# Expert stage of a GNN + MoE kernel: the fetch of output rows waits for the scatter ahead of it only where a table says so

## The chip, the cores and the metric

The kernel runs on one core of one Trainium2 chip. The metric is the device time of one execution in microseconds (us). The engines are PE (matmul), DVE (vector), ACT (scalar), POOL (GpSimd) and SP (SyncE, which here only issues transfers). Each has its own instruction queue, worked off in order. Queues wait for each other through semaphores; a transfer raises its semaphore by 16 when it has landed.

## The reference

```python
x = x + _L0_gnn_ref(_layernorm(x), edge_index, ...)      # graph attention, 3125 nodes, 50000 edges
x = x + _L0_ffn_ref(_layernorm(x)[None], ...)[0]
# _L0_ffn_ref: x [3125, 1024] float32, E = 8 experts, F = 512, top_k = 2
top_v, top_i = jax.lax.top_k(gate_scores, top_k)
gate_probs = jax.nn.softmax(top_v, axis=-1)
comb = jnp.sum(jax.nn.one_hot(top_i, E) * gate_probs[..., None], axis=-2)
h = jax.nn.gelu(jnp.einsum('bsd,edf->ebsf', x, W1) + b1[:, None, None, :], approximate=False)
eo = jnp.einsum('ebsf,efd->ebsd', h, W2) + b2[:, None, None, :]
out = jnp.einsum('ebsd,bse->bsd', eo, comb)
```

Each node goes to exactly two different experts, and the two results, weighted by their gates, are added to its row.

## The kernel before

The first two thirds of the time are the graph layer. Then a routing block sorts the 6250 pairs (node, expert) by expert and pads every expert to a multiple of 128 slots, at least one tile. There are XTILES = 56 tiles of P = 128 slots. `tokT` holds the node of every slot (3125 and above for an empty one, which the transfers skip), `gateT` its gate. A chain of small DVE steps on one partition (lines 1454 to 1482) makes a table `x_i` with a column per tile: row 0 a word with the tile's expert and flags (first tile of an expert, and so on), rows 1 to 3 further numbers. An engine reads an entry into a register with `tile_value` (line 1534).

The expert stage (from line 1515) runs over the 56 tiles in order. Tile i has parity p = i % 2, and i = 2j + p; most buffers are double by parity. What each queue does for a tile:

- SP (line 1563 on): loads the tile's output bias, broadcast to 128 partitions (`b_t`, 512 KB, line 1569), and, once for each of the later experts, the weights of the expert three ahead (`w_f`, two transfers of 2 MB, line 1286), when the buffer is free.
- POOL, in `body`: `gather(i + 2)` (lines 1271 to 1280) copies a column of node numbers to `xi` and issues the indirect load of 128 normed rows; `put(i - 1)` waits until DVE is done with tile i - 1 and issues the indirect scatter of its 128 rows of 4 KB to `out` (line 1594); `fetch(i)` waits for the scatter of tile i - 1 to land, copies the node numbers (line 1586) and issues the indirect load of the 128 rows of `out` into `y[p]` (line 1588).
- PE: `first(i)` (24 matmuls of 512 columns, line 1695), the first half of `second(i - 1)` (12, line 1710), the turning of the gathered input of tile i + 1 (line 1762), the second half of `second(i - 1)` (12), the turning of h (line 1721).
- ACT: gelu (line 1656), the high half of h (1658), the copy of the turned input (1648) and of the turned h (1664); at an expert's first two tiles also two pieces each of the high half of new weights (1293).
- DVE: bias on h (line 1628), the low half of h (1631), then `take(i - 1)`: `x_o = x_o / 64 + b_t` (line 1618) and `y = x_o * gate + y` (line 1621); at an expert's first two tiles also two pieces each of the low half of new weights (1300).

A fetch must see what an earlier scatter wrote to the same row. Within one expert every node has at most one slot; a row that tile i fetches was written by a neighbouring tile only if that tile belongs to another expert. The semaphores are `s_st[p]` (scatters of parity p), `s_y[p]` (fetches), `s_eo` (takes), `s_tr` (inputs turned). `wait_apart` (line 118 on) gives a wait an instruction of its own.

The lines that the change works on:

```python
def fetch(i, j, p):
    if not early(i, 1):
        wait_apart(pool, s_met, s_st[1 - p], 16 * (j + p))
    pool.tensor_copy(xi[:, 2 + p, :], at1(tokT, i)).then_inc(s_xo, 1)
    wait_apart(pool, s_met, s_xo, i + 1)
    pool.indirect_dma_start(out=y[:, p, :], ..., in_=out[:, :], ...).then_inc(s_y[p], 16)
```

Of the kernel before, what the change touches and what calls it, by code (L numbers as in the profile page):

```python
# [31 lines left out]
I32 = mybir.dt.int32  # L32
U32 = mybir.dt.uint32
F16 = mybir.dt.float16
ALU = mybir.AluOpType
# [22 lines left out]
XTILES = (PAIRS + NX * P - 1) // P  # L58
# [37 lines left out]
def early(i, n):  # L96

    return isinstance(i, int) and i < n
# [19 lines left out]
def wait_apart(eng, met, sem, value):  # L118


    if not isinstance(value, int):
        eng.lower_val(value)
    eng.wait_ge(met, 1)
    eng.wait_ge(sem, value)
# [42 lines left out]
def program(nc, x, src, dst, W, att_src, att_dst, bias, Wp, sim, temp, W1, b1, W2, b2, out):  # L167
# [12 lines left out]
    ctx = ExitStack()  # L180
# [4 lines left out]
    def sbuf(c, name, shape, dt=F32):  # L185
        return c.enter_context(nc.sbuf_tensor(name, shape, dt))
# [4 lines left out]
    s_met = sem("always_met")  # L191

    with ctx:
# [18 lines left out]
        gateT = sbuf(ctx, "gate_of_slot", [P, XTILES])  # L212


        x_i = sbuf(ctx, "tile_experts", [1, 4, XTILES], I32)


        edge_ctx = ExitStack()
# [1083 lines left out]
        with ExitStack() as c:  # L1302
# [18 lines left out]
            base = sbuf(c, "base", [ROWS, NX, BLOCKS + 1])  # L1321
# [10 lines left out]
            slot_f = sbuf(c, "slot_f", [ROWS, 2, BLOCKS])  # L1332
            dif = sbuf(c, "dif", [ROWS, 3, BLOCKS])
            tile_r = sbuf(c, "tile_r", [1, XTILES])
            xcmp = sbuf(c, "xcmp", [1, XTILES, NX - 1])
            xe_f = sbuf(c, "xe_f", [1, XTILES + 1])
            x_t = sbuf(c, "x_t", [1, 5, XTILES + 1])
# [10 lines left out]
            with nc.Block() as block:  # L1348
# [7 lines left out]
                @block.gpsimd  # L1356
                def _(pool):
                    pool.memset(strict[:, :], 1.0).then_inc(s_k, 1)
                    pool.iota(block_of[:, :], pattern=[[0, 2], [1, BLOCKS]], base=-BLOCKS, channel_multiplier=0,
                              allow_small_or_imprecise_dtypes=True).then_inc(s_k, 1)  # L1360
                    pool.iota(tile_r[:, :], pattern=[[P, XTILES]], base=0, channel_multiplier=0,
                              allow_small_or_imprecise_dtypes=True).then_inc(s_k, 1)
                    pool.wait_ge(s_k, 3)
                    pool.affine_select(out=strict[:, :], in_=strict[:, :], compare_op=ALU.is_gt, fill=0.0, base=0,
                                       pattern=[[1, ROWS]], channel_multiplier=-1).then_inc(s_k, 1)
                    pool.wait_ge(s_tok, 1)
                    gather(pool, 0, 0)
                    gather(pool, 1, 1)
# [13 lines left out]
                def _(dve):  # L1382
# [60 lines left out]
                    dve.tensor_tensor(in_tile, iota16[0:ROWS, 0:XTILES].unsqueeze(1).broadcast_to([ROWS, PLACES, XTILES]),  # L1443
                                      slot_p[:, 0, :].unsqueeze(2).broadcast_to([ROWS, PLACES, XTILES]), ALU.is_equal).then_inc(s_tile, 1)
                    dve.wait_ge(s_tile, 1)
                    dve.wait_ge(s_k, 4)
                    dve.tensor_tensor(at_tile[:, :, 0, :], in_tile,
                                      block_of[:, :].unsqueeze(2).broadcast_to([ROWS, PLACES, XTILES]), ALU.mult).then_inc(s_part[0], 1)
                    for n in range(2):
# [22 lines left out]
                    dve.tensor_tensor(x_t[:, 0, now], xe_f[:, now], xe_f[:, ago], ALU.not_equal)  # L1472
                    dve.tensor_scalar(ahead[:, :], xe_f[:, :], float(NX - 3), None, ALU.is_lt)
                    link(dve.tensor_scalar(x_t[:, 1, now], xe_f[:, now], float(NX - 2), None, ALU.is_lt))
                    link(dve.tensor_tensor(first[:, now], x_t[:, 0, now], x_t[:, 1, now], ALU.mult))
                    dve.memset(ahead[:, 0:1], 0.0)
                    link(dve.tensor_tensor(ahead[:, now], first[:, now], ahead[:, now], ALU.mult))
# [19 lines left out]
                @block.tensor  # L1497
                def _(pe):
                    pe.wait_ge(s_oh, 1)
                    pe.wait_ge(s_k, 4)  # L1500
                    flat = both[:, :, :].rearrange("r b e -> r (b e)")
                    pe.matmul(b_ps[0:ROWS, 0, 0:BLOCKS * NX], ones[0:ROWS, 0:ROWS], flat, start=True, stop=True).then_inc(s_mm, 1)
                    pe.matmul(b_ps2[0:ROWS, 0, 0:BLOCKS * NX], strict[:, :], flat, start=True, stop=True).then_inc(s_mm, 1)

                    for n, to in enumerate((inv_ps, gate_ps)):
                        for part in s_part[2 * n:2 * n + 2]:
                            pe.wait_ge(part, 1)
                        for j in range(PLACES):
                            if n == 0 and j % BLOCKS == 0:
                                pe.wait_ge(s_row, j // BLOCKS + 1)  # L1510
                            ins = pe.matmul(to[:, 0:2 * XTILES], at_row[:, j, :], at_tile[:, j, 2 * n:2 * n + 2, :], start=(j == 0), stop=(j == PLACES - 1))
                        ins.then_inc(s_inv, 1)


        with expert_ctx, ExitStack() as c:
# [17 lines left out]
            def tile_value(eng, n, i, **bounds):  # L1533
                return eng.value_load(x_i[:, n, i:i + 1] if isinstance(i, int) else x_i[:, n, bass.ds(i, 1)], **bounds)
# [27 lines left out]
            with nc.Block() as block:  # L1562
# [18 lines left out]
                def _(pool):  # L1581
                    def fetch(i, j, p):

                        if not early(i, 1):
                            wait_apart(pool, s_met, s_st[1 - p], 16 * (j + p))
                        pool.tensor_copy(xi[:, 2 + p, :], at1(tokT, i)).then_inc(s_xo, 1)  # L1586
                        wait_apart(pool, s_met, s_xo, i + 1)
                        pool.indirect_dma_start(out=y[:, p, :], out_offset=None, in_=out[:, :],
                                                in_offset=bass.IndirectOffsetOnAxis(ap=xi[:, 2 + p, :], axis=0),
                                                bounds_check=NODES - 1, oob_is_err=False).then_inc(s_y[p], 16)  # L1590
# [220 lines left out]
```

## Time and profile before

| | |
|---|---|
| median of 3 runs | 2454.21 us |
| lowest, highest | 2448.95, 2456.05 us |
| the profiled execution, its own time | 2455.99 us |
| its span, first to last instruction | 2454.2 us |
| mean granted TensorE clock | 0.903 of full speed |
| PE, DVE, ACT, POOL busy | 2006.4 (82%), 1517.5 (62%), 1115.4 (45%), 709.3 (29%) us |
| moved by transfers | 489.14 MB, 199 GB/s on average |

The time is that of the whole execution, the span what the profile covers of it. Busy time is time in which an engine works on an instruction; instructions that only wait, branch, load a register or issue a transfer from SP are not counted. The granted clock is the share of the full TensorE clock that the chip allows at a time: it has two levels, 1.2 and 2.4 GHz. The chain that ended last is followed back from the last instruction, at each step to what released it. In a timeline, the text in brackets is how long the engine had been idle before the instruction and what ended the wait. A transfer issued by POOL shows as a DMA_INDIRECT of about 1 us, the time that POOL's engine needs to issue it; its landing is seen in what waits for it.

### The profile page before, as it was taken

What the parts mean: (1) busy time and instruction counts of PE and PEld (TensorE: products, weight loads), DVE (VectorE), ACT (ScalarE), POOL (GpSimd) and SP (SyncE); (2) the same over time, 40 slices, a digit from 0 to 9 for tenths busy, and PEclk for the clock granted to TensorE, in tenths of its full rate; (3) what the DMA queues carried; (4) which work ended last, traced back from release to release, by engine and by line L of the source; (5) the groups of instructions that cost most, each with busy time, mean ns of one, the idle gap of its engine ahead of it and who ended that gap; (6) DMA issues with size and microseconds to landing.
All of it is one profiled execution on the core that took longest, in us unless ns stands there. A gap on an engine that the chain in (4) does not pass through costs nothing. (4 is left out here: it accounts for less than half of the span.)

```text
span 2454.2 us, 53610 instructions
## 1 busy us (share of the span) xinstructions
PE 2006.4 (82%) x14842; PEld 1337.3 (54%) x14843; DVE 1517.5 (62%) x4463; ACT 1115.4 (45%) x2399; POOL 709.3 (29%) x933
## 2 busy tenths in 40 slices
PE   2888897666669999999999387773898999999997
PEld 1455555444438787878888255442344444444553
DVE  3776674777767777777777678877533433433332
ACT  2333432111128787878787355541533433433332
POOL 0002000000016666666665001001222332333332
PEclk9899898555689999999999689995899999999999
DMA  3533344233019999999999455545545546545442
GB/s 131 170 101 112 111 140 138 97 129 123 0 56 353 363 343 362 346 348 354 344 354 333 150 180 184 184 149 189 222 166 215 216 149 216 202 159 168 162 170 80
DMA packets 141057, 489.14 MB, mean 199 GB/s; under 512 B 22449, under 2 KB 22659, under 8 KB 138829
## 3 DMA queue, kind: packets, MB, share of 16 engines
q0 software_dynamic: 98912, 346.99, 40.3%
q1 hardware_dynamic: 41853, 140.70, 15.9%
q8 instruction: 48, 0.79, 0.1%
q10 hardware_dynamic: 216, 0.43, 0.0%
q14 instruction: 28, 0.23, 0.0%
HBM read 418.06 MB, written 81.27 MB: 203 GB/s over the span
## 5 line engine op out<-in xcount | busy, mean ns | idle before, releaser
L1035 PE MATMUL main_ps<-rows,O 128*128 128x256 f16 x4992 | 576.5, 274 | 49.7 <-DVE acc L974 28.6
L1021 ACT ACTIVATE O<-O,pk 128x128 f16<-128x128 f16 x1664 | 499.5, 387 | 126.0 <-DVE O L991 124.3
L1035 PEld LDWEIGHTS main_ps<-rows,O 128*128 128x128 f16 x4992 | 463.7, 98 | 120.1 <-DVE acc L974 33.7
L960 POOL DMA_INDIRECT rows<-projected,idx x416 | 394.6, 948 | 199.5 <-issue 83.7
L1744 PE MATMUL pj_ps<-gram,xsT 128*125 128x512 f16 x1200 | 292.6, 405 | 46.0 <-ACT xsT L396 45.3
L995 DVE TENSOR_SCALAR O<-O,pk 128x128 f16<-128x128 f16 x1664 | 319.2, 270 | 14.9 <-DVE O L991 0.2
L1695 PE MATMUL x_h<-w_p,gram 128*128 x1344 | 309.1, 388 | 17.1 <-ACT gram L1648 11.3
L1710 PE MATMUL x_o<-w_p,gram 128*128 x1344 | 310.8, 382 | 1.4 <-ACT gram L1664 1.4
L1744 PEld LDWEIGHTS pj_ps<-gram,xsT 128*125 128x125 f16 x1200 | 171.0, 146 | 155.8 <-ACT xsT L396 53.5
L1695 PEld LDWEIGHTS x_h<-w_p,gram 128*128 128x128 f16 x1344 | 132.3, 100 | 171.9 <-issue 33.2
L1753 PE MATMUL n_pj<-gram,PK 128*128 128x512 f16 (+3 forms) x900 | 166.5, 344 | 62.1 <-ACT PK L1226 62.1
L1710 PEld LDWEIGHTS x_o<-w_p,gram 128*128 128x128 f16 x1344 | 130.0, 98 | 149.2 <-issue 5.1
L1656 ACT ACTIVATE h_g<-h_b 128x512 f32<-128x512 f32 x56 | 35.3, 630 | 347.4 <-DVE h_b L1628 347.4
L1753 PEld LDWEIGHTS n_pj<-gram,PK 128*128 128x128 f16 x900 | 87.1, 103 | 137.6 <-ACT PK L1226 66.4
L1621 DVE SCALAR_TENSOR_TENSOR x_y<-x_o,gate_of_slot,x_y 128x1024 f32<-128x1024 f32 x56 | 71.9, 1284 | 145.7 <-DMA x_y<-out_dram,xi 143.4
L991 DVE TENSOR_SCALAR O<-iota,pk 128x128 f16<-128x128 f16 x416 | 114.1, 274 | 58.9 <-DVE pk L984 30.9
L1618 DVE SCALAR_TENSOR_TENSOR x_o<-x_o,b_t 128x1024 f32<-128x1024 f32 x56 | 69.0, 1232 | 129.2 <-PE x_o L1710 108.9
L1594 POOL DMA_INDIRECT out_dram<-x_y,xi x56 | 68.5, 1223 | 245.0 <-DVE x_y L1621 245.0
L1648 ACT ACTIVATE gram<-x_tr 128x2048 f16<-128x2048 f16 x56 | 104.7, 1869 | 63.8 <-PE x_tr L1762 63.5
L955 POOL COPY idx<-srcT 128x4 int32 (+1 forms) x104 | 21.2, 203 | 317.9 <-SPq L947 313.3
L755 ACT ACTIVATE d_p<-d_ps 128x64 f32 (+1 forms) x104 | 23.2, 223 | 186.3 <-PE d_ps L782 186.3
L369 POOL DMA_DIRECT2D projected_f<-xp_f x25 | 13.2, 527 | 297.9 <-ACT xp_f L390 297.9
(332 smaller groups left out, 2619.2 us busy)
## 6 DMA issues: line engine op xcount, KB each, us to landing
w_f<-in_L_ffn_W_dram SPq DMA_DIRECT2D x14, 2048.0 KB, 12.9
b_t<-in_L_ffn_b_dram SPq DMA_DIRECT2D x56, 512.0 KB, 4.7
xt<-in_x_dram SPq DMA_DIRECT2D x25, 500.0 KB
projected_f<-xp_f POOLq DMA_DIRECT2D x25, 500.0 KB, 3.7
projected<-xp POOLq DMA_DIRECT2D x25, 500.0 KB, 4.8
n_own<-projected_f SPq DMA_DIRECT2D x25, 500.0 KB
n_xt<-in_x_dram SPq DMA_DIRECT2D x25, 500.0 KB
out_dram<-n_x POOLq DMA_DIRECT2D x25, 500.0 KB, 9.9
```

The source lines that it names most:

```text
L960: pool.indirect_dma_start(out=rows[:, 4 * p + k, :, :].rearrange("k n d -> k (n d)"), out_offset=None, in_=xp_d[:, :], in_offset=bass.Indi ...
L991: dve.tensor_scalar(O[:, k, 0, :], iota16[:, :], pk[:, p, k, 0:1], None, ALU.is_equal).then_inc(s_oh, 1)
L995: ins = dve.tensor_scalar(O[:, k, 1 + h, :], O[:, k, 0, :], pk[:, p, k, 1 + h:2 + h], None, ALU.mult)
L1021: ins = act.activation(O[:, k, 1 + HEADS + h, :], O[:, k, 0, :], ACT.Copy, scale=pk[:, p, k, w:w + 1])
L1035: pe.matmul(main_ps[:, h * C:(h + 1) * C], O[:, k, 1 + HEADS * a + h, :], rows[:, 4 * p + k, b, h * C:(h + 1) * C], start=first and h % 2 ...
L1618: dve.scalar_tensor_tensor(o_ps[:, p, :], o_ps[:, p, :], 1.0 / WS, b2_t[:, p, :], ALU.mult, ALU.add).then_inc(s_ob, 1)
L1621: dve.scalar_tensor_tensor(y[:, p, :], o_ps[:, p, :], at1(gateT, i), y[:, p, :], ALU.mult, ALU.add).then_inc(s_eo, 1)
L1648: act.activation(xgT[:, p, :, :, :], tr_ps[:, :, :, :], ACT.Copy).then_inc(s_xT, 1)
L1695: ins = pe.matmul(h_ps[:, :], xgT[:, p, a, k, :], w, start=(k == 0 and a == b), stop=(k == KD - 1 and a == 1))
L1710: ins = pe.matmul(o_ps[:, p, n * 512:(n + 1) * 512], hT[:, p, a, f, :], w, start=(f == 0 and a == b), stop=(f == KF - 1 and a == 1))
L1744: ins = pe.matmul(out, lhs[:, a, k, :], rhs[:, b, k, :], start=(k == 0 and a == b), stop=(k == last - 1 and a == 1))
L1753: ins = pe.matmul(out[:, cols], lhs[:, a, k, :], rhs[:, b, k, cols], start=(k == 0 and a == b), stop=True, skip_group_check=True)
```

## The change

The table gets a fifth row: for each tile a count, 16 times the number of scatters of the other parity that must have landed before its fetch is issued. At the first tile of an expert this is the scatter of the tile just ahead; at other tiles it is the one before that of the same parity, three tiles ahead; the count is never less than 16. `fetch` now waits in two places. Ahead of the copy it waits for the scatter two tiles ahead, which frees the `y` buffer. Behind the copy it waits for the count from the table, read into a register. Tiles 0 and 1 have waits written out.

```diff
--- before.py
+++ after.py
@@ -212,7 +212,7 @@
         gateT = sbuf(ctx, "gate_of_slot", [P, XTILES])
 
 
-        x_i = sbuf(ctx, "tile_experts", [1, 4, XTILES], I32)
+        x_i = sbuf(ctx, "tile_experts", [1, 5, XTILES], I32)
 
 
         edge_ctx = ExitStack()
@@ -1332,6 +1332,8 @@
             slot_f = sbuf(c, "slot_f", [ROWS, 2, BLOCKS])
             dif = sbuf(c, "dif", [ROWS, 3, BLOCKS])
             tile_r = sbuf(c, "tile_r", [1, XTILES])
+            put_r = sbuf(c, "put_r", [1, XTILES])
+            put_n = sbuf(c, "put_n", [1, XTILES])
             xcmp = sbuf(c, "xcmp", [1, XTILES, NX - 1])
             xe_f = sbuf(c, "xe_f", [1, XTILES + 1])
             x_t = sbuf(c, "x_t", [1, 5, XTILES + 1])
@@ -1360,7 +1362,9 @@
                               allow_small_or_imprecise_dtypes=True).then_inc(s_k, 1)
                     pool.iota(tile_r[:, :], pattern=[[P, XTILES]], base=0, channel_multiplier=0,
                               allow_small_or_imprecise_dtypes=True).then_inc(s_k, 1)
-                    pool.wait_ge(s_k, 3)
+                    pool.iota(put_r[:, :].rearrange("a (j p) -> a j p", p=2), pattern=[[16, XTILES // 2], [16, 2]], base=-16, channel_multiplier=0,
+                              allow_small_or_imprecise_dtypes=True).then_inc(s_k, 1)
+                    pool.wait_ge(s_k, 4)
                     pool.affine_select(out=strict[:, :], in_=strict[:, :], compare_op=ALU.is_gt, fill=0.0, base=0,
                                        pattern=[[1, ROWS]], channel_multiplier=-1).then_inc(s_k, 1)
                     pool.wait_ge(s_tok, 1)
@@ -1443,7 +1447,7 @@
                     dve.tensor_tensor(in_tile, iota16[0:ROWS, 0:XTILES].unsqueeze(1).broadcast_to([ROWS, PLACES, XTILES]),
                                       slot_p[:, 0, :].unsqueeze(2).broadcast_to([ROWS, PLACES, XTILES]), ALU.is_equal).then_inc(s_tile, 1)
                     dve.wait_ge(s_tile, 1)
-                    dve.wait_ge(s_k, 4)
+                    dve.wait_ge(s_k, 5)
                     dve.tensor_tensor(at_tile[:, :, 0, :], in_tile,
                                       block_of[:, :].unsqueeze(2).broadcast_to([ROWS, PLACES, XTILES]), ALU.mult).then_inc(s_part[0], 1)
                     for n in range(2):
@@ -1472,6 +1476,8 @@
                     dve.tensor_tensor(x_t[:, 0, now], xe_f[:, now], xe_f[:, ago], ALU.not_equal)
                     dve.tensor_scalar(ahead[:, :], xe_f[:, :], float(NX - 3), None, ALU.is_lt)
                     link(dve.tensor_scalar(x_t[:, 1, now], xe_f[:, now], float(NX - 2), None, ALU.is_lt))
+                    link(dve.scalar_tensor_tensor(put_n[:, :], x_t[:, 0, now], 16.0, put_r[:, :], ALU.mult, ALU.add))
+                    dve.tensor_scalar(x_i[:, 4, :], put_n[:, :], 16.0, None, ALU.max)
                     link(dve.tensor_tensor(first[:, now], x_t[:, 0, now], x_t[:, 1, now], ALU.mult))
                     dve.memset(ahead[:, 0:1], 0.0)
                     link(dve.tensor_tensor(ahead[:, now], first[:, now], ahead[:, now], ALU.mult))
@@ -1497,7 +1503,7 @@
                 @block.tensor
                 def _(pe):
                     pe.wait_ge(s_oh, 1)
-                    pe.wait_ge(s_k, 4)
+                    pe.wait_ge(s_k, 5)
                     flat = both[:, :, :].rearrange("r b e -> r (b e)")
                     pe.matmul(b_ps[0:ROWS, 0, 0:BLOCKS * NX], ones[0:ROWS, 0:ROWS], flat, start=True, stop=True).then_inc(s_mm, 1)
                     pe.matmul(b_ps2[0:ROWS, 0, 0:BLOCKS * NX], strict[:, :], flat, start=True, stop=True).then_inc(s_mm, 1)
@@ -1581,10 +1587,15 @@
                 def _(pool):
                     def fetch(i, j, p):
 
-                        if not early(i, 1):
-                            wait_apart(pool, s_met, s_st[1 - p], 16 * (j + p))
+                        if not early(i, 2):
+                            puts = tile_value(pool, 4, i, min_val=16, max_val=8 * XTILES)
+                            wait_apart(pool, s_met, s_st[p], 16 * j)
                         pool.tensor_copy(xi[:, 2 + p, :], at1(tokT, i)).then_inc(s_xo, 1)
                         wait_apart(pool, s_met, s_xo, i + 1)
+                        if not early(i, 2):
+                            wait_apart(pool, s_met, s_st[1 - p], puts)
+                        elif i == 1:
+                            wait_apart(pool, s_met, s_st[0], 16)
                         pool.indirect_dma_start(out=y[:, p, :], out_offset=None, in_=out[:, :],
                                                 in_offset=bass.IndirectOffsetOnAxis(ap=xi[:, 2 + p, :], axis=0),
                                                 bounds_check=NODES - 1, oob_is_err=False).then_inc(s_y[p], 16)
```

## Rows read from the trace of the kernel before

**Rows 1.** The page's chain that ended last, by line: shares of the span.
```profile
DMA x_y<-out_dram,xi 6%; DMA out_dram<-x_y,xi 5%; PE x_h L1695 5%; PE x_o L1710 5%; DVE x_y L1621 2%; PE x_tr L1762 1%; DVE w_p L1300 1%; PE x_ht L1721 0%; POOL xi L1586 0%; DMA gram<-x_after_gnn_normed,xi 0%; ACT w_p L1293 0%; DVE x_o L1618 0%; ACT gram L1648 0%; ACT h_g L1656 0%; DVE h_b L1628 0%
```

**Rows 2.** Timeline of PE, tiles 3, 50, 55: start, length, engine, line.
```profile
1765.84 5.35 PE L1695 MATMUL x_h<-w_p,gram 128*128 x24 [0.70 <-ACT gram L1648]
...
2366.36 5.34 PE L1695 MATMUL x_h<-w_p,gram 128*128 x24
...
2424.86 5.34 PE L1695 MATMUL x_h<-w_p,gram 128*128 x24
```

**Rows 3.** Stretch: length, PE PEld DVE ACT POOL busy, PEclk, DMA, GB/s.
```profile
1765.80:2424.90 659.10, 625.42 (x3745) 317.58 (x3746) 245.45 (x228) 249.74 (x228) 200.66 (x258) 0.98 0.53 184
```

**Rows 4.** Waits, PE and POOL, 1765.8 to 2424.9: us, times, longest.
```profile
PE x_tr L1762 <- DMA gram<-x_after_gnn_normed,xi: 16.2, 10, 3.9
PE x_h L1695 <- ACT gram L1648: 10.6, 16, 1.0
PE x_ht L1721 <- DVE h_s L1631: 7.1, 5, 2.7
...
POOL xi L1586 <- DMA out_dram<-x_y,xi: 155.5, 52, 7.4
```

**Rows 5.** Timeline of DVE and POOL, take of tile 4 to tile 5.
```profile
1808.50 1.28 DVE L1621 SCALAR_TENSOR_TENSOR x_y<-x_o,gate_of_slot,x_y 128x1024 f32<-128x1024 f32 x1 [6.31 <-DMA x_y<-out_dram,xi]
...
1810.67 1.03 POOL L1594 DMA_INDIRECT out_dram<-x_y,xi  x1 [4.74 <-DVE x_y L1621]
...
1814.23 0.18 POOL L1586 COPY xi<-token_of_slot 128x1 int32 x1 [2.54 <-DMA out_dram<-x_y,xi]
...
1815.28 1.04 POOL L1588 DMA_INDIRECT x_y<-out_dram,xi  x1 [0.87 <-POOL xi L1586]
...
1817.36 1.01 POOL L1277 DMA_INDIRECT gram<-x_after_gnn_normed,xi  x1 [0.84 <-POOL xi L1275]
...
1821.20 1.28 DVE L1621 SCALAR_TENSOR_TENSOR x_y<-x_o,gate_of_slot,x_y 128x1024 f32<-128x1024 f32 x1 [6.32 <-DMA x_y<-out_dram,xi]
```

**Rows 6.** The same timeline, PE at tile 7.
```profile
1814.55 5.35 PE L1695 MATMUL x_h<-w_p,gram 128*128 x24 [0.59 <-ACT gram L1648]
```

**Rows 7.** Timeline of DVE and POOL, quiet end of the stage.
```profile
2355.96 1.28 DVE L1621 SCALAR_TENSOR_TENSOR x_y<-x_o,gate_of_slot,x_y 128x1024 f32<-128x1024 f32 x1 [0.22 <-DVE x_o L1618]
...
2362.79 1.09 POOL L1588 DMA_INDIRECT x_y<-out_dram,xi  x1 [0.87 <-POOL xi L1586]
...
2367.66 1.28 DVE L1621 SCALAR_TENSOR_TENSOR x_y<-x_o,gate_of_slot,x_y 128x1024 f32<-128x1024 f32 x1 [0.21 <-DVE x_o L1618]
```

**Rows 8.** Line 1534, register loads on PE: ns min/median/max.
```profile
L1534 PEldq TENSOR_LOAD <-tile_experts x57: 297/301/1178, 1716.8 to 2433.2; - x57
```

**Rows 9.** Line 1480, DVE in the table's chain: ns min/median/max.
```profile
L1480 DVE SCALAR_TENSOR_TENSOR x_t<-x_t x4: 205/206/206, 1699.5 to 1700.2; 1x56 f32<-1x56 f32 x4
```

**Rows 10.** Timeline of SP, POOL, DVE beside expert 4's weights.
```profile
1853.15 1.01 SPq L1286 DMA_DIRECT2D w_f<-in_L_ffn_W_dram  x2
...
1853.88 1.03 POOL L1588 DMA_INDIRECT x_y<-out_dram,xi  x1 [0.87 <-PE x_tr L1762]
...
1862.77 1.28 DVE L1621 SCALAR_TENSOR_TENSOR x_y<-x_o,gate_of_slot,x_y 128x1024 f32<-128x1024 f32 x1 [5.43 <-DMA x_y<-out_dram,xi]
...
1871.89 1.23 DVE L1618 SCALAR_TENSOR_TENSOR x_o<-x_o,b_t 128x1024 f32<-128x1024 f32 x1 [4.46 <-DMA b_t<-in_L_ffn_b_dram]
1872.79 0.18 POOL L1586 COPY xi<-token_of_slot 128x1 int32 x1 [6.81 <-DMA out_dram<-x_y,xi]
```

**Rows 11.** Timeline of PE and DVE, splits of tiles 21, 22.
```profile
2015.12 5.34 PE L1695 MATMUL x_h<-w_p,gram 128*128 x24
...
2018.82 4.49 DVE L1300 SCALAR_TENSOR_TENSOR w_p<-w_f,w_p 128x2048 f32 x2 [1.13 <-ACT w_p L1293]
...
2027.35 5.35 PE L1695 MATMUL x_h<-w_p,gram 128*128 x24 [0.37 <-ACT gram L1648]
...
2039.84 1.03 PE L1695 MATMUL x_h<-w_p,gram 128*128 x4 [0.62 <-ACT gram L1648]
```

## The prediction

> **What bounds the kernel now.** I read the summary of the chain of waits first: of its whole-span shares the largest are the fetch of output rows (x_y<-out_dram, 6%), their scatter (5%) and the two matmul groups of the expert stage (5% each) [rows 1]. So that stage alternates between a loop of transfers and PE. The matmuls of line 1695 tell how often: 24 belong to one tile, 56 tiles. Tile 3 starts at 1765.84, tile 50 at 2366.36 and tile 55 at 2424.86 [rows 2]. The last five take 58.50 / 5 = 11.70 us each, and PE has no gap in them: that is PE's pace. At it, the 52 tiles from 3 to 55 need 608.4 us; they took 659.0. **The excess is 50.6 us, and it is all that any change to the transfers can win here.** The table by stretch and PE's waits account for it: PE was busy 625.4, 17.0 more than 608.4, since the mean granted clock was 0.98 and not 1.00 (part of the time at 1.2 instead of 2.4 GHz, after PE had idled) [rows 3], and it waited 16.2 for gathered inputs, 10.6 for ACT's copy of the turned input and 7.1 for DVE's low half of h [rows 4]: 33.9 + 17.0 = 50.9.
>
> **Whose fault these waits are.** Follow one tile in order of time [rows 5]. The final DVE step of line 1621 ("the take") of tile 4 starts at 1808.50 and ends at 1809.78. POOL issues its scatter at 1810.67 (0.89 later), sits idle 2.54 until it has landed, copies the row numbers at 1814.23, issues the fetch of tile 5 at 1815.28, and 5.92 later the next take starts, 6.32 us after DVE was free. Loop: 1821.20 - 1808.50 = 12.70, against PE's 11.70. The gather of tile 8 is queued on POOL behind that fetch, at 1817.36, so it is late with it, and DVE's h_b of line 1628 is queued behind the take: take, h_b, then ACT's steps, then PE's tile 7 at 1814.55, which waited for ACT [rows 6]: 4.77 us after the take ended. All three of PE's waits are thus mostly children of a late take. In the quiet end of the stage the same distance is 2366.36 - 2357.24 = 9.12 [rows 2, 7], so there a take can be 9.12 - 4.77 = **4.35 us late before PE notices**.
>
> **The change part by part.** (1) *The wait removed.* Fetch now starts scatter + 4.61 (1815.28 - 1810.67) [rows 5]. Without the wait the order on POOL is scatter issue, copy, fetch issue. The trace has this very sequence in the pair behind it: fetch issue 1815.28, copy, gather issue 1817.36, 2.08 apart. With a few more semaphore steps I take 2.2. So each relaxed fetch leaves 2.4 us earlier. The gather queued behind it gains the same 2.4.
> (2) *The wait kept.* By the table, the first tile of an expert waits as now. Experts hold about 6250 / 8 = 781 slots, 7 tiles, so tiles 7, 14, 21 and so on wait; tiles 1 and 2 do too (tile 1 by the code, tile 2 because the count is not let below 16). Their loop in a quiet stretch shows the cost: fetch at 2362.79, and the take starts 0.21 after the step of line 1618 ahead of it, so the fetch was down within 4.7 and cost PE nothing [rows 7]. I charge these tiles 0. Other tiles wait for the scatter two and three ahead, which lands a whole tile earlier: 0.
> (3) *The register load added on POOL* once a tile. No row shows one on POOL. On PE's sequencer it takes 297 to 301 ns, once 1178 [rows 8]. It stands behind the scatter's issue, and that keeps POOL's engine for 1.03 us, so I take 0 on the path; bounds 0 (hidden) and 1.2 (the longest, exposed). Even 1.2 of the 2.4 leaves a loop below PE's pace. The Trainium skill (DMA: Bandwidth & Descriptors, Latency and other measured facts) puts the floor of a tensor_load at about 600 ns; the rows show half of that on PE; by 600 ns the load would still end inside the scatter's issue, and the sum is the same.
> (4) *The table.* DVE gets one linked scalar_tensor_tensor and one unlinked tensor_scalar on 1x56, in a chain without gaps ahead of the gathers: 0.206 us for the first by its like [rows 9], and no more for the second, which reads as much: at most 0.5 with their wake-ups, at least 0.2. **+0.3 us.** POOL's extra iota is done 30 us before its reader: 0; uncovered it would be 0.2.
> (5) *The fetch beside the scatter.* Now they would overlap: the fetch starts 2.2 after the scatter, which lands at about 3.35 (1.03 issue + 2.54 idle, less the wake-up) [rows 5]. The flight of a fetch shown is 5.92 from issue to take beside a b_t load, at most 4.7 in the quiet stretch [rows 5, 7] and 8.89 beside expert weights [rows 10]. I take it as unchanged. Bounds: 0, and the 1.15 us that the scatter has left.
>
> **New loop**: 0.89 + 2.2 + 5.92 + 1.28 (take) = 10.3; with 1.15 for overlap and 1.2 for the load 12.6, above PE's pace but still below today's. At my value it is 1.4 under 11.70, so PE sets the pace of all ordinary tiles, and lateness heals by 1.4 a tile.
>
> **What is late next.** *Splitting of weights.* For each of experts 3 to 7, two pairs of DVE pieces (line 1300, 4.49 us a pair [rows 11]) go between a take and the next h_b. At tiles 21 and 22 this stood alone, PE having had no wait before it: tile 22 starts at 2015.12, tile 23 at 2027.35 and 24 at 2039.84, that is 12.23 and 12.49, or 0.53 + 0.79 = 1.32 us [rows 11]. The change doesn't touch it: 5 x 1.32 = 6.6 us stay.
> *The weight loads.* SP issues 4 MB for experts 4 to 7 once each, at 1853.15 the first time (for expert 4). Beside it the fetch of tile 8 took 8.89, the scatter kept POOL idle 6.81, and the b_t of tile 9, behind 4 MB in SP's queue, held DVE until 1871.89, 18.74 after the issue [rows 10]. Put T for the end of tile 7's take; the load comes after the second pair, about T + 5.6. The fetch of tile 8 leaves at T + 3.1, 2.5 us ahead of the load, where it now leaves behind it. Tile 9's fetch: take of tile 8 at T + 11.7, fetch T + 14.8, landed T + 23.7. Tile 9's b_t: T + 24.3, so b_t ends last. Its line-1618 step is due at T + 20.7 (23.4 less 2.72, its own 1.23 [rows 10], 0.21 and the take's 1.28 [rows 7]): 3.6 late, or 2.8 once PE is 0.8 behind by the split. That is below 4.35, and the next tiles heal it. PE stalls 0 by this, but several transfers can slip together: I take 1.5 us a load, bounds 0 and 5, four loads: 6 us.
>
> **Sum.** 50.6 - 6.6 - 6.0 = 38.0 gained, 0.3 given for the table: net 37.7. What follows tile 55's start is left as it is. The profiled execution took 2455.99 (span 2454.2), 1.8 above the median of the runs, 2454.21. 2455.99 - 37.7 = 2418.3; less that 1.8, **2416.5 us**.
>
> **Rivals.**
> A, the forecast: PE sets the pace, 5 to 20 us of the excess stay. 2405 to 2425; 0.66.
> B, the fetch gets through only behind the scatter. For it: both are in one software queue, and both stretch to 7 or 9 us beside weights [rows 10]. Mechanism: the fetch's data start when the scatter has landed, so only its issue is hidden: saved are the 1.26 us between landing and issue. A quiet loop is then 11.4 and still PE's. But beside a load tile 9 has 11.7 + 0.9 + 7.6 + 8.9 + 1.3 = T + 30.4 against a due T + 23.4, 7 late, 2.7 over the slack, with lost clock and a late gather about 5 us for each of four loads. 20 us instead of 6: 2430, up to 2436. 0.20. The skill has this rule (DMA: Bandwidth & Descriptors, Two DMAs through the same engine are not ordered): within one queue of an engine descriptors start in order, but are pipelined. It bears on this case only in its milder form; no row of before has a scatter and a fetch in flight together.
> C, slower. Place: the pair in flight, written rows against read rows of the same tensor. If they hinder each other as weights hinder them, every fetch takes 8.9: 0.89 + 2.2 + 8.9 + 1.28 = 13.3 a tile, 52 tiles: 690 against 659, 2485. It decides from a flight of 8.3 on (12.67 mean now, less 4.37). Against it: gather and fetch, issued 2.08 apart, run side by side today at 5.9. 0.04.
> D, no relaxation in fact: the table's entries too high, or POOL's register wait eats the 2.4. The formula gives 16(j + p) at a first tile and 16 less elsewhere, so for it speaks only the unseen POOL load; exposed it would have to cost 2.4, twice the longest row. 2454 within 7; 0.04. Some other mishap with a gain over 50 or below 18: 0.06, mostly still faster.
>
> **Numbers.** A and B hold 0.86; cutting their outer ends, 8 in 10 gives 2403 to 2436. 2403 is the whole excess gone (2454.2 - 50.6 = 2403.6). Over 0.3% (7 us, about what can be told from no change here) faster: A, B and most of the rest, 0.92; within: 0.05; slower: 0.03.
>
> **What would show it.** Right: PE's starts of line 1695 are 11.70 apart but for two per expert; the copy of line 1586 follows the scatter's issue at once and its wait of 155.5 us [rows 4] is nearly gone; fetch issue 2.2 after scatter issue except at first tiles; PE's wait for gathers under 4 us; the chain goes through PE for over 80% of the stage. The step on overlap is wrong if a fetch's flight grows by over 1.2 in quiet stretches; the one on loads if PE's gaps at tiles 10 to 12 and 17 to 19 stay over 3 us. The forecast is wrong if tiles still run at 12 or more.

## The result and the profile after

The changed kernel took **2424.36 us** (median of 4 runs, 2422.76 to 2426.14) against 2451.78 for the kernel before in the same runs: ratio 0.9888, 95% interval 0.9875 to 0.9901, 27.4 us less. The forecast was 2416.5, range 2403 to 2436, with 37.7 us gained. A second set of runs gave 0.9869 (0.9852 to 0.9886), 31.0 us less. So the direction and the mechanism held, and the size fell 7 to 10 us short.

The chain that ended last, by line, of the changed kernel (against [rows 1]; lines of the expert stage now stand about 11 higher):

```profile
PE x_h L1706 8%; PE x_o L1721 8%; DMA b_t<-in_L_ffn_b_dram 3%; PE x_tr L1773 1%; DVE w_p L1300 1%; ACT gram L1659 1%; ACT w_p L1293 1%; PE x_ht L1732 1%; ACTq L1540 0%; DVE h_b L1639 0%; ACT h_g L1667 0%; DVE x_o L1629 0%; DVEq L1540 0%; SPq L1286 0%; DVE x_y L1624 0%
```

The scatter is gone from it and the fetch too; PE's two matmul groups have 8% each instead of 5%, and a newcomer has 3%: the bias rows b_t. PE's first matmul groups of tiles 3, 50 and 55 (against [rows 2]), and the busy time of that stretch (against [rows 3]):

```profile
1770.92 1.46 PE L1706 MATMUL x_h<-w_p,gram 128*128 x3 [0.75 <-ACT gram L1659]
...
2336.83 5.34 PE L1706 MATMUL x_h<-w_p,gram 128*128 x24
...
2395.33 1.03 PE L1706 MATMUL x_h<-w_p,gram 128*128 x4
```

```profile
1770.90:2395.40 624.50, 613.36 (x3745) 314.87 (x3746) 246.94 (x228) 250.79 (x228) 206.15 (x258) 1.00 0.56 194
```

From tile 3 to tile 55 it is 624.4 us; before it was 659.0, and PE's pace makes 608.4. 34.6 us were won here and 16.0 are left. The granted clock is back at 1.00, PE's busy time only 5.0 over 608.4. The waits of that stretch (against [rows 4]: us in total, times, longest):

```profile
DVE x_o L1629 <- DMA b_t<-in_L_ffn_b_dram: 40.5, 5, 9.6
...
DVE x_y L1632 <- DMA x_y<-out_dram,xi: 31.6, 11, 4.5
...
POOL x_y L1599 <- DMA out_dram<-x_y,xi: 9.7, 5, 2.9
...
PE x_h L1706 <- ACT gram L1659: 8.7, 13, 1.0
...
PE x_ht L1732 <- DVE h_s L1642: 2.3, 3, 1.5
...
PE x_tr L1773 <- DMA gram<-x_after_gnn_normed,xi: 0.9, 2, 0.7
```

The same view of DVE in the kernel before:

```profile
DVE x_y L1621 <- DMA x_y<-out_dram,xi: 142.6, 44, 7.3
...
DVE x_o L1618 <- DMA b_t<-in_L_ffn_b_dram: 20.3, 5, 6.5
```

POOL's wait for the scatter fell from 155.5 us to 9.7, PE's for gathers from 16.2 to 0.9. DVE's wait for fetches fell from 142.6 us to 31.6, but its wait for bias rows rose from 20.3 to 40.5. POOL and DVE in a quiet stretch (against [rows 5, 7]), the register load on POOL (against [rows 8]), and the flight of the 56 fetches:

```profile
2340.30 1.03 POOL L1605 DMA_INDIRECT out_dram<-x_y,xi  x1 [4.97 <-DVE x_y L1632]
2341.34 0.19 POOL L1593 COPY xi<-token_of_slot 128x1 int32 x1
...
2342.39 1.04 POOL L1599 DMA_INDIRECT x_y<-out_dram,xi  x1 [0.86 <-issue]
...
2344.46 1.00 POOL L1277 DMA_INDIRECT gram<-x_after_gnn_normed,xi  x1 [0.84 <-POOL xi L1275]
...
2349.84 1.28 DVE L1632 SCALAR_TENSOR_TENSOR x_y<-x_o,gate_of_slot,x_y 128x1024 f32<-128x1024 f32 x1 [0.22 <-DVE x_o L1629]
```

```profile
L1540 POOLq TENSOR_LOAD <-tile_experts x54: 285/288/490, 1772.9 to 2409.4; - x54
```

```profile
DMA to landing us min/median/max: 2.1/4.4/10.2
```

Scatter issue 2340.30, copy behind it without a gap, fetch issue 2342.39: 2.09 us. The take at 2349.84 waits 0.22 for the step ahead of it and not for the fetch. The register load takes 0.288 us on POOL's sequencer and runs beside the scatter's issue of 1.03. The median flight of a fetch is 4.4, which is what it was before (median 4.4, longest 8.8); only the longest grew, to 10.2.

### The profile page after: what moved, and what is told of

It is laid out like the page before. It is cut to its first block and busy times, and to the rows that moved or that the text cites. A ratio compares the mean times of both kernels' runs of the same rounds, so it can differ in the third digit from the quotient of the medians.

```text
span 2424.4 us, 53856 instructions
## 1 busy us (share of the span) xinstructions
PE 2000.9 (83%) x14842; PEld 1337.6 (55%) x14843; DVE 1517.8 (63%) x4465; ACT 1116.3 (46%) x2399; POOL 715.9 (30%) x935
## 5 line engine op out<-in xcount | busy, mean ns | idle before, releaser
L1021 ACT ACTIVATE O<-O,pk 128x128 f16<-128x128 f16 x1664 | 499.1, 387 | 126.0 <-DVE O L991 124.7
L1605 POOL DMA_INDIRECT out_dram<-x_y,xi x56 | 57.5, 1027 | 352.4 <-DVE x_y L1632 348.1
L1639 DVE SCALAR_TENSOR_TENSOR h_b<-x_h,b_b 128x512 f32<-128x512 f32 x56 | 38.6, 690 | 111.0 <-PE x_h L1706 106.7
```

The costliest lines, as they stand in the source:

```text
L1021: ins = act.activation(O[:, k, 1 + HEADS + h, :], O[:, k, 0, :], ACT.Copy, scale=pk[:, p, k, w:w + 1])
L1605: pool.indirect_dma_start(out=out[:, :], out_offset=bass.IndirectOffsetOnAxis(ap=xi[:, 2 + p, :], axis=0), in_=y[:, p, :], in_offset=None, ...
```

## The experiments

All ratios are to the kernel before, run beside it in the same set of runs. Beside them stands the stretch from PE's tile 3 to tile 55 in the profile, written "stage": it leaves out what earlier stages do by chance.

**1. table_only.** Is the late entry to the stage the table's price?

```diff
 def fetch(i, j, p):
-    if not early(i, 2):
-        puts = tile_value(pool, 4, i, ...)
-        wait_apart(pool, s_met, s_st[p], 16 * j)
+    if not early(i, 1):
+        wait_apart(pool, s_met, s_st[1 - p], 16 * (j + p))
...
-    if not early(i, 2):
-        wait_apart(pool, s_met, s_st[1 - p], puts)
-    elif i == 1:
-        wait_apart(pool, s_met, s_st[0], 16)
```

> The changed kernel with the old wait in the fetch put back; the table is still computed, and nobody reads its fifth row. Open is why the profiled execution of the changed kernel reached tile 3 about 5.1 us later than before. Theory (the table costs two DVE steps, the rest was chance of that execution): 0.3 to 0.6 us slower than before, ratio 1.000, routing block longer by 0.5 at most. Rival (the table or the extra iota costs it each time): 3 to 5 us slower, ratio 1.0012 to 1.002.

2451.7 against 2452.47 us, ratio 1.0002 (0.9990 to 1.0014). PE's tile 3 starts at 1765.42, against 1765.84 before and 1770.92 in the changed kernel, and from the start of the routing block to PE's first tile it is 59.5 us, where two profiles of the kernel before have 59.3 and 59.6. The table costs nothing that can be told from zero, and the rival (3 to 5 us) is out. The stage took 651.2 us in this profile, though its code is that of before but for line numbers: 8 less than in the execution that the forecast was made against.

**2. counted_all.** All waits kept, but by the new code.

```diff
-link(dve.scalar_tensor_tensor(put_n[:, :], x_t[:, 0, now], 16.0, put_r[:, :], ALU.mult, ALU.add))
+link(dve.tensor_scalar(put_n[:, :], put_r[:, :], 16.0, None, ALU.add))
```

> The changed kernel with every entry of the table raised to the count of the tile just ahead: all waits of before are kept, but they are taken behind the copy of the row numbers and against a register. Theory (the register load hides behind the scatter's issue, the copy now lies beside the scatter's flight): fetch issue 4.15 us after scatter issue where it was 4.61, so 0.4 us a tile on some 25 tiles whose pace the transfer loop sets: 3 to 12 us faster than before, ratio 0.995 to 0.999, and far from the changed kernel's 0.989. Rival (the load or the register wait costs time on POOL): fetch issue 4.9 or more after the scatter, slower than before, ratio over 1.002.

2445.71 us, ratio 0.9971 (0.9960 to 0.9982), 6.8 less than before. The stretch from tile 3 to 55, and one scatter with its fetch:

```profile
1768.60:2412.00 643.40, 618.95 (x3745) 318.21 (x3746) 246.06 (x228) 251.75 (x228) 202.34 (x258) 0.98 0.56 188
```

```profile
1888.86 1.03 POOL L1605 DMA_INDIRECT out_dram<-x_y,xi  x1 [5.19 <-DVE x_y L1632]
1889.89 0.20 POOL L1593 COPY xi<-token_of_slot 128x1 int32 x1
1893.12 1.49 POOL L1599 DMA_INDIRECT x_y<-out_dram,xi  x1 [3.04 <-DMA out_dram<-x_y,xi]
```

The copy now runs beside the scatter's flight, and the fetch leaves 4.26 us after the scatter's issue where it was 4.61 [rows 5]. So the register wait costs no more than 0.1 (4.15 was expected), and putting the copy ahead of the wait is worth 0.35 where the scatter lands at once; in the median of all tiles the distance fell from 4.83 to 4.60. Some 7 of the 27 us can be had by this reordering alone; the relaxation gives the rest.

**3. all_free.** Do the waits kept at an expert's first tile cost anything?

```diff
-        wait_apart(pool, s_met, s_st[1 - p], puts)
...
-    pool.indirect_dma_start(out=y[:, p, :], ..., in_=out[:, :],
+    pool.indirect_dma_start(out=y[:, p, :], ..., in_=own_d[:, :],
...
 if not early(i, 1):
+    if not early(i, 2):
+        wait_apart(pool, s_met, s_st[p], 16 * j)
     put(i - 1, 1 - p)
```

> The changed kernel with no wait of a fetch for the scatter ahead of it at any tile, the expert's first included; the fetch reads the rows of another tensor of the same shape (the projected rows in float32) so that nothing depends on the scatter. Leaves out: what was in the output rows before. Theory (the waits kept at first tiles are covered by PE): within 2 us of the changed kernel, ratio 0.988 to 0.989. Rival (the kept waits are part of the 16 us by which PE still misses its pace): 4 to 10 us faster than the changed kernel, ratio 0.985 to 0.987.

2424.53 us, ratio 0.9885 (0.9869 to 0.9900): as the changed kernel. Its stage is even 4 us longer:

```profile
1766.40:2395.10 628.70, 615.21 (x3745) 315.07 (x3746) 246.95 (x228) 250.57 (x228) 208.12 (x258) 0.99 0.57 193
```

The 4 us are not due to the waits. The bias rows of tile 2, which stand in SP's queue behind expert 3's weights (issued at 1762.57), held DVE until 1784.79:

```profile
1784.79 1.23 DVE L1625 SCALAR_TENSOR_TENSOR x_o<-x_o,b_t 128x1024 f32<-128x1024 f32 x1 [10.04 <-DMA b_t<-in_L_ffn_b_dram]
```

PE then waited 2.1 us in tile 4 and took 1.6 us longer for tile 5, at a granted clock of 0.88; the gaps beside the later loads add up to 10.0 instead of 8.4. In the changed kernel itself the take of tile 7, whose fetch waited, is on time (the line at 1844.06 in the next section), and PE has no gap near tiles 41 and 48, the first tiles without a split beside them. Kept waits cost nothing that these runs can tell, as the forecast charged them. Without register load and table wait the fetch leaves 2.06 behind the scatter here, with them 2.09. (The fetch reads another tensor here, so this speaks for the waits, not for reads and writes of one tensor.)

**4. small_loads.** What do the weight loads cost?

```diff
-load_weights(sp, e_ago + 3, w_f, s_w)
+for n, w in enumerate((W1, W2)):      # 128 columns of the first block of rows only
+    ...
```

> The changed kernel with the weight loads of experts 4 to 7 cut from two transfers of 2 MB to two of 64 KB each. Leaves out: the right weights of those experts. Theory (the bias rows that stand behind 4 MB in SP's queue, and transfers slowed beside it, cost PE about 8.4 us over four loads): 7 to 10 us faster than the changed kernel, ratio to before about 0.985, PE's gaps of 2.3, 1.0, 2.3 and 2.8 us near tiles 12, 19, 26 and 33 gone, the splits' gaps of 0.5 to 0.9 still there. Rival (the splits of weights on DVE and ACT alone make these gaps): under 2 us faster.

2415.22 us, ratio 0.9847 (0.9833 to 0.9861), 9.3 less than all_free, which ran beside it. (The edit leaves out most of the weights of five experts and not four: expert 3's load, at 1764 us, is cut too. In the changed kernel that one cost PE nothing.) The stage:

```profile
1768.00:2384.10 616.10, 611.44 (x3745) 315.13 (x3746) 247.65 (x228) 251.72 (x228) 204.36 (x258) 1.00 0.50 163
```

616.0 us, 8.4 less than the changed kernel's 624.4. The gaps at tiles 12, 19, 26 and 33 are gone, and the eight splits' gaps of 0.6 to 0.9 remain. So of the 16.0 us left, **8.4 belong to the loads, 5.9 to the splits, 1.6 to a low clock at tile 3.**

**5. after_again.** The changed kernel again.

> The changed kernel once more, on the chip and in the call of the kernels below, so that they can be held against it. Both theories: ratio 0.9885 within 0.0015. Open is also whether its late entry to the expert stage was chance: theory, PE's first tile starts 59.7 us after the routing block as in the other runs, and the routing block starts anywhere from 1662 to 1668; rival, it starts at 1668 again.

Ratio 0.9869, stage 624.5 us against 624.4, and the same gaps within 0.5 us. The routing block started at 1661.8 instead of 1667.9, so the late entry was chance, ahead of the stage and of the table. Over the ten profiles on chips of the usual speed it starts anywhere from 1661.8 to 1668.6. In the first profile the extra came from the stage ahead, whose granted clock was 0.86 and PE's busy time 223.95 us, where the kernel before had 0.89 and 219.03:

```profile
1341.00:1656.60 315.60, 223.95 (x1925) 147.71 (x1923) 232.17 (x513) 154.07 (x221) 26.80 (x51) 0.86 0.49 170
```

**6. bias_ahead.** SP issues the next tile's bias rows ahead of the load.

```diff
 def body(i, j, p):
-    e, _, _, _, _, ahead = tile_word(sp, i)
-    if not early(i, 2):
-        wait_apart(sp, s_met, s_ob, i - 1)
-    sp.dma_start(b2_t[:, p, :], ...e...)
+    _, _, _, _, _, ahead = tile_word(sp, i)
+    e_next = tile_word(sp, i + 1)[0]
+    if not early(i, 1):
+        wait_apart(sp, s_met, s_ob, i)
+    bias(i + 1, 1 - p, e_next)
     ...                             # then the weight load, if this tile has one
```

> The changed kernel with SP issuing the output bias of the next tile ahead of this tile's weight load, so that the bias rows of the load's second tile no longer stand behind 4 MB in SP's queue. Theory (the bias rows are what makes the take late beside a load, with the fetch only just ahead of them): DVE's wait for bias rows falls from 40 us to under 12, the wait for fetches grows by 5 to 10, and the time falls by 1 to 4 us against the changed kernel. Rival (the transfers as a whole are short of bandwidth beside a load, whichever is first): the fetch lands as late as the bias rows did, under 1 us gained.

2416.63 us, ratio 0.9847 (0.9832 to 0.9863), 3.5 less than after_again's 2420.14. Waits:

```profile
DVE x_y L1638 <- DMA x_y<-out_dram,xi: 42.6, 14, 5.1
...
PE x_h L1712 <- ACT gram L1665: 5.4, 9, 0.8
```

DVE's wait for bias rows is not merely short but gone; that for fetches rose from 33.3 in after_again to 42.6. The stage took 616.9, 7.6 less, and of PE's gaps beside the loads only one of 0.8 is left, at tile 33. The theory holds. The 3.5 us of the medians is less than the stage gives, and single runs of the two kernels overlap.

**7. copy_early.** POOL copies the row numbers before it waits for the take.

```diff
+if not early(i, 2):
+    wait_apart(pool, s_met, s_st[p], 16 * j)
+pool.tensor_copy(xi[:, 2 + p, :], at1(tokT, i)).then_inc(s_xo, 1)
 if not early(i, 1):
     put(i - 1, 1 - p)
 fetch(i, j, p)                      # without wait and copy of its own
```

> The changed kernel with POOL's copy of the row numbers moved ahead of the wait for the take and the scatter, where POOL idles. In the changed kernel the copy of the load's first tile took 2.12 us beside DVE's split of weights and the fetch's issue another 2.21, so that the fetch left behind the weight load instead of ahead of it. Theory (that delay is part of why the forecast's step on loads failed): fetch issue 1.1 to 1.9 us after scatter issue, the fetch of tile 8 ahead of the load, PE's gaps near tiles 12, 19, 26 and 33 shorter by 1 to 2 us each, 2 to 6 us faster than the changed kernel. Rival (the fetch's place does not matter, the bias rows end last anyway): within 1.5 us of it.

2421.01 us, ratio 0.9865 (0.9848 to 0.9883): no different from the changed kernel in time. Fetch issue did move to 1.35 us behind the scatter's, and the stage took 621.0, 3.5 less. The fetch of tile 8 leaves at 1847.51, 4.1 us ahead of the load, and DVE's wait for fetches fell from 33.3 to 10.8; but the bias rows still held DVE until 1872.66, and their wait stayed at 41.4. PE's gaps beside the loads fell from 8.4 to 5.0. By the measured times the rival holds, by the profile the theory in part; alone it is not settled.

**8. both.** Experiments 6 and 7 together.

> Both of the above together: bias rows ahead of the load, copy ahead of the take. Theory (two causes in a row, each hiding the other): 5 to 8 us faster than the changed kernel, PE's gaps near tiles 12, 19, 26 and 33 under 0.5 us each, which leaves the splits' 5.9. Rival (bandwidth beside the load is what is short): under 3 us faster.

2411.36 us, ratio 0.9833 (0.9819 to 0.9848), 8.8 less than the changed kernel and 5.3 less than bias_ahead alone. Waits, and the first loaded tile:

```profile
DVE x_y L1639 <- DMA x_y<-out_dram,xi: 10.9, 6, 4.4
...
PE x_h L1713 <- ACT gram L1666: 5.3, 9, 0.8
```

```profile
1844.28 2.65 POOL L1603 DMA_INDIRECT x_y<-out_dram,xi  x1 [0.32 <-issue]
...
1848.40 1.02 SPq L1286 DMA_DIRECT2D w_f<-in_L_ffn_W_dram  x2
...
1853.03 1.28 DVE L1639 SCALAR_TENSOR_TENSOR x_y<-x_o,gate_of_slot,x_y 128x1024 f32<-128x1024 f32 x1 [0.21 <-DVE x_o L1636]
```

The fetch of tile 8 leaves at 1844.28, 4.1 us ahead of the load at 1848.40, and the take at 1853.03 is on time, where in the changed kernel it was held until 1860.47. Stage 614.5: 608.4, the splits' 5.9 and 0.2 of low clock. With the bias rows out of the way the fetch was next in line, but for PE little hung on it: of the 2.4 us between bias_ahead's stage and this one the copy's place accounts for the gap of 0.8 at tile 33, and the other 1.5 is the low clock at tile 3, which bias_ahead had and this profile has not. The medians' 5.3 is more than the stage can show.

**9. bias_ahead_before.** The same edit of SP on the kernel before.

> The kernel before with SP issuing the next tile's output bias ahead of the weight load, and every scatter wait as it was. Open is whether the bias rows cost anything by themselves or only once the wait for the scatter is gone. Theory (before, the fetch was the later one of the two nearly everywhere, DVE waited 142.6 us for fetches and 20.3 for bias rows): within 2 us of before to 4 us faster, ratio 0.9985 to 1.000, less than the 0.0022 it brought on top of the change. Rival (independent causes): 5 us faster or more, ratio 0.998 or less.

2546.69 against 2556.0 us, ratio 0.9957 (0.9940 to 0.9973): 9.3 us, and the stage 645.8 against 653.1. **My theory fell**: the edit is worth about as much without the change as on top of it, 7.3 us of the stage against 7.6. (The medians' 9.3 against 3.5 does not show that it is worth more: the intervals of the two gains overlap.) In before_again DVE waited 22.9 us for bias rows and 126.0 for fetches, here not at all for bias rows and 135.3 for fetches. So what the bias rows cost was not hidden behind the waits for fetches; why not was not tried by itself.

**10. both_again.** 

> Bias rows ahead of the load and copy ahead of the take, once more, to be held against the next kernel. Ratio 0.9833 within 0.0015.

2521.57 us, ratio 0.9858 (0.9837 to 0.9880), stage 615.2. The ratio is higher than expected, 34.4 us gained instead of 39.8; as a stage it agrees within 0.7 us. This set ran on a chip on which every kernel was 100 us slower (last section).

**11. both_spread.** DVE's pieces one by one in its idle times.

```diff
 dve.tensor_tensor(h_s[:, 1, :], ...)            # low half of h
+if not early(i, 2):
+    with dve.If(flag_ago == 1): piece(i, 1)
+if not early(i, 3):
+    with dve.If(tile_word(dve, i - 1)[4] == 1): piece(i - 1, 3)
 take(i - 1, ...)
-split(dve, low, i, e, flag, flag_ago)           # two pieces, at two tiles
+with dve.If(flag_ago == 1): piece(i, 2)
+with dve.If(flag == 1): low(dve, [0], e + 2, q)
```

> The same with DVE's four pieces of low halves per expert spread over its idle times: one behind the take of the first tile, one behind the low half of h and one behind the take of the second, one behind the low half of h of the third. Theory (what PE still misses, 5.9 us over ten gaps of 0.5 to 0.9, is h_b waiting behind two pieces in a row): the ten gaps gone, 4 to 6 us faster than without, ratio to before about 0.981. Rival (the gaps come from ACT, whose high pieces and copy of the turned input stand in a row as well): under 2 us faster, gaps in place.

2513.93 us against both_again's 2521.57 in the same set, ratio to before 0.9825 (0.9804 to 0.9847). DVE around the second and third tile of an expert:

```profile
2107.83 2.29 DVE L1300 SCALAR_TENSOR_TENSOR w_p<-w_f,w_p 128x2048 f32 x1 [1.38 <-issue]
...
2113.65 2.33 DVE L1300 SCALAR_TENSOR_TENSOR w_p<-w_f,w_p 128x2048 f32 x1 [0.89 <-ACT w_p L1293]
2115.90 0.68 DVE L1651 SCALAR_TENSOR_TENSOR h_b<-x_h,b_b 128x512 f32<-128x512 f32 x1
...
2120.69 2.29 DVE L1300 SCALAR_TENSOR_TENSOR w_p<-w_f,w_p 128x2048 f32 x1 [2.06 <-issue]
...
2126.77 0.69 DVE L1651 SCALAR_TENSOR_TENSOR h_b<-x_h,b_b 128x512 f32<-128x512 f32 x1 [1.16 <-PE x_h L1732]
```

A piece ahead of the bias step, one behind the take (2113.65) that delays h_b to 2115.90, one in the next tile's gap. All of the splits' gaps of 0.5 to 0.9 are gone (they were eight, not ten as I had written), which confirms their cause. The stage took 612.2, 3.0 less; of the 3.8 left 1.6 are again a low clock at tile 3, and 2.2 are gaps beside three of the loads (1.2 at tile 33), which both_again did not have. By the stage the theory's 4 to 6 us are not reached. The medians say 7.6, more than the stage can give; I count 3. **This is the fastest version tried**, on its chip 42.1 us under before, where the changed kernel's own gain was 27 to 31.

**12. before_again.**

> The kernel before once more, one look. The profiled execution that the sum was made against took 659.0 us from tile 3 to tile 55, while the same code with a table that nobody reads took 651.2. Theory (executions of the kernel before differ by several us in this stage, because its pace hangs on transfers, while the changed kernel's 624.4 and 624.5 agree): some value from 648 to 660 that is not 659.0. Rival (the table's place in memory or code changes the stage): 659 again within 1.

```profile
1871.30:2524.60 653.30, 622.35 (x3745) 318.09 (x3746) 245.49 (x228) 250.39 (x228) 200.50 (x258) 0.98 0.54 185
```

653.1 us. So the three profiles of the loop as it was give 659.0, 653.1 and 651.2, and the two of the changed kernel 624.4 and 624.5.

## Why the prediction was right, and where its size was off

The account of the profiled pair: stage -34.6, tiles 0 to 3 +1.3, routing block with the table +0.4, all ahead of it +3.5, end -0.3: -29.8 us of span, from 2454.2 to 2424.4.

- *The bound and the removed wait* (1): right. Fetch 2.09 behind the scatter (forecast 2.2), PE at 11.70 on every quiet tile, POOL's wait for the scatter gone. Two things the step left out. The copy moved ahead of the wait helps the tiles that still wait (counted_all): 3.5 to 4.15 at experts' first tiles, where it was 4.5 to 6.2. And at experts' second tiles, beside a split, the relaxed fetch leaves not 2.2 but 3.8 to 4.0 behind the scatter.
- *Kept waits* (2): right, all_free. (The last two experts start at tiles 41 and 48, not 42 and 49; it made no difference.)
- *Register load* (3): right, 0.288 us, hidden. The Trainium skill's floor of about 600 ns for a tensor_load (DMA: Bandwidth & Descriptors, Latency and other measured facts) is twice what POOL shows, and by either the sum is the same.
- *Table* (4): 0.4 in one pair of profiles, within what the same code varies by; nothing by the times.
- *Fetch beside scatter* (5), and rival C: right, median flight 4.4 in both. Rival B, strict order behind the scatter, has no trace in quiet tiles. Beside loads the longest flight grew, 10.2 for 8.8. More bytes then share one stretch: from 1851 to 1876 the transfers moved 7.86 MB, before 6.71 MB from 1853 to 1872. That this is what lengthened it was not tried by itself.
- *Splits*: 6.6 said, 5.9 found: the experts at tiles 14 and 28 show one gap of 0.9 and not two.
- *Loads*: 6.0 said, 8.4 found. **This step failed in size, and in two of its sentences.** Its working gave a stall of 0, and the 1.5 us a load was an allowance on top; that 6.0 came as near to 8.4 as it did is partly luck. "The fetch of tile 8 leaves at T + 3.1, 2.5 us ahead of the load": it left at T + 4.9, 1.5 us ahead (not behind the load, as the expectation of experiment 7 has it). POOL, DVE, SP and PE at the first loaded tile of the changed kernel:

```profile
1844.06 1.28 DVE L1632 SCALAR_TENSOR_TENSOR x_y<-x_o,gate_of_slot,x_y 128x1024 f32<-128x1024 f32 x1 [0.23 <-DVE x_o L1629]
...
1847.04 4.49 DVE L1300 SCALAR_TENSOR_TENSOR w_p<-w_f,w_p 128x2048 f32 x2 [1.70 <-ACT w_p L1293]
1847.26 2.12 POOL L1593 COPY xi<-token_of_slot 128x1 int32 x1
...
1850.24 2.21 POOL L1599 DMA_INDIRECT x_y<-out_dram,xi  x1 [0.86 <-issue]
...
1851.71 1.01 SPq L1286 DMA_DIRECT2D w_f<-in_L_ffn_W_dram  x2
...
1860.47 1.28 DVE L1632 SCALAR_TENSOR_TENSOR x_y<-x_o,gate_of_slot,x_y 128x1024 f32<-128x1024 f32 x1 [4.34 <-DMA x_y<-out_dram,xi]
...
1874.19 1.23 DVE L1629 SCALAR_TENSOR_TENSOR x_o<-x_o,b_t 128x1024 f32<-128x1024 f32 x1 [9.05 <-DMA b_t<-in_L_ffn_b_dram]
...
1881.56 3.62 PE L1706 MATMUL x_h<-w_p,gram 128*128 x16 [0.94 <-ACT gram L1659]
```

POOL's copy took 2.12 us beside DVE's split, the fetch's issue 2.21, and the load came at 1851.71; the take came 10.23 after the fetch's issue. I had costed POOL's steps from a tile without splits. And "tile 9's b_t: T + 24.3": b_t held DVE until 1874.19, 22.5 us after the load's issue and not 18.7. T, the end of tile 7's take, is 1845.34, so that is T + 28.85. It was due at T + 20.7, or T + 22.05 with PE's two split gaps of 0.58 and 0.79: 6.8 us late, 2.45 over the slack of 4.35, and PE lost 2.3 before it started tile 12 at 1881.56. Of the two the second weighs more. Edits show it: with the bias rows ahead (bias_ahead) PE's gaps beside the loads fall from 8.4 to 0.8, and moving the copy as well (both) takes out that 0.8. The copy alone (copy_early) brings them to 5.0. The step also counted four loads, from 1853.15 on, and overlooked expert 3's, at 1767.02 in the changed kernel: its bias rows held DVE 5.1 us there and cost PE nothing, but in all_free they did.
- *The base.* This is the largest part of the miss. The excess of 50.6 us was read off one execution. Two more of the same loop had 44.7 (653.1) and 42.8 (651.2, with the table), so some 6 to 8 us of the forecast gain were that execution's own. I said how it stood to the median by its whole time, 1.8 us; against the median of 23 later runs, 2452.47, it was 3.5 above. Against 651 to 653 the stage after gives a gain of 27 to 29, which is what the times show.
- *Low clock at tile 3*, 1.6 us: not in the sum. Both profiles of the changed kernel have it (granted clock 0.88 in that tile), as have those of table_only, counted_all, small_loads, bias_ahead, copy_early and both_spread; both of before, both of the kernel of experiment 8, all_free and bias_ahead_before do not. There the low stretch fell on tile 2 (0.89, PE busy 13.7 us instead of 12.0), which takes 15.4 either way because PE waits in it. The three kernels that were profiled twice repeated themselves, table_only shares its loop with before and differs; so what decides it is open.
- *The sign that failed*: the chain in this stage goes through PE for 64%, not over 80; the bias rows have 13%. The other signs came true: 11.70 on quiet tiles, PE's wait for gathers 0.9, no gap over 3 beside a load.

Together: of the 10.3 us by which 27.4 fell short of 37.7, loads 2.4, low clock 1.6, splits -0.7, and some 7 of the base.

## What to carry to other kernels

Before removing a wait, work out how late the consumer may be before the bounding engine notices (4.35 us here), and spend that slack on the tiles with the largest transfers: the wait removed in quiet tiles was worth all it promised, and most of what was left came from a small transfer that stood behind a bulk load in the same queue. Issue the small transfer that the next tile needs ahead of the bulk load (7.6 us of the stage here); address copies on POOL before it starts waiting came second. Read the excess off two or three executions, or give the base a range of its own: the loop paced by transfers varied by 8 us over three profiles, where the two kernels paced by PE and profiled twice repeated within 0.1 and 0.7.

## What was unexpected of the hardware

- A copy of 128 numbers on POOL, 0.19 us otherwise, took 2.12 beside DVE's split step (line 1300), and the issue of an indirect transfer 2.21 instead of 1.03. In the kernel before the copy was issued later and took up to 1.66.
- On the chip of the last set (experiments 9 to 12) every kernel ran some 100 us slower. The expert stage was the same (653.1 us before). The difference lies in the graph layer, in the stretch 720 to 1341, where the kernel before moved 348 GB/s on the first chip and PE was busy 571.34 us of 621:

```profile
720.00:1341.00 621.00, 512.38 (x4559) 430.59 (x4557) 404.84 (x1994) 423.85 (x1403) 355.44 (x445) 0.97 0.88 299
```

299 GB/s (the last column) and 512.38 us there, so that this stretch took longer; why is not shown. A ratio measured on such a chip is diluted by the stage that the change does not touch, but only a little: the 39.8 us of experiment 8 would be a ratio of 0.9844 there, and 0.9858 was measured.
- Bias rows queued behind weights slowed a kernel whose takes waited for fetches anyway: DVE's wait for them was 20 to 23 us in the kernel before, and taking it away gained 9.3, or 7.3 of the stage.
